# Two-layer decoder, state-space stage: side work of ScalarE and VectorE placed by half units

## The reference, cut to what matters

```python
for i in range(nl):                                  # 4
    h = _rms(x, norm_w[i])
    xz = jnp.einsum('bld,ed->ble', h, W_in[i])
    xi, z = jnp.split(xz, 2, axis=-1)
    xp = jnp.pad(xi, ((0, 0), (dc - 1, 0), (0, 0)))
    xc = conv_b[i] + sum((xp[:, k:k + L, :] * conv_w[i][:, k] for k in range(dc)))
    xc = _silu(xc)
    dbc = jnp.einsum('bld,ed->ble', xc, W_x[i])
    delta, Bm, Cm = jnp.split(dbc, [rk, rk + n], axis=-1)
    delta = jax.nn.softplus(jnp.einsum('blr,dr->bld', delta, W_dt[i]) + b_dt[i])
    A = -jnp.exp(A_log[i])
    deltaA = jnp.exp(delta[..., None] * A)
    BX = (delta * xc)[..., None] * Bm[:, :, None, :]
    _, hs = jax.lax.associative_scan(combine, (deltaA, BX), axis=1)
    y = jnp.einsum('bldn,bln->bld', hs, Cm) + D[i] * xc
    out = jnp.einsum('bld,ed->ble', y * _silu(z), W_out[i])
    x = x + out
```

## Time and profile before

| what | value |
|---|---|
| median of 3 runs | 1283.86 us (1282.17 to 1284.41) |
| the profiled execution, its own time | 1286.74 us |
| span of its profile | 1285.0 us |
| busy share of the span: PE, DVE, ACT, POOL | 88%, 82%, 64%, 60% |
| mean granted TensorE clock | 0.949 of full speed |

### The profile page before, as it was taken

The page is one execution under the profiler, slowest core; times in us unless marked ns, Lnnn a source line. Parts: engine busy times, 40 slices in busy tenths (PEclk is TensorE's granted clock), DMA queues, the critical chain, the costliest instruction groups (busy, mean ns, idle before and its releaser), DMA issues.

```text
span 1285.0 us, 17476 instructions
## 1 busy us (share of the span) xinstructions
PE 1128.5 (88%) x5960; PEld 660.0 (51%) x5960; DVE 1050.3 (82%) x1642; ACT 825.1 (64%) x1816; POOL 775.4 (60%) x641
## 2 busy tenths in 40 slices
PE   7798888879759998998998999989989689999974
PEld 3455555544325454554554545545545346666643
DVE  4577777675689999999999999999999985676657
ACT  1455555655466786777767767877776436788763
POOL 6001111100389898998998999989989952554202
PEclk9899999998979999999998999989999899999878
DMA  7000002000510600502404107014042003100000
GB/s 211 13 13 13 13 13 73 2 1 3 201 44 0 217 34 2 205 17 88 162 1 181 42 1 251 1 54 168 1 150 88 1 11 90 34 18 18 2 1 26
DMA packets 22141, 79.13 MB, mean 62 GB/s; under 512 B 4935, under 2 KB 8847, under 8 KB 21138
## 3 DMA queue, kind: packets, MB, share of 16 engines
q1 hardware_dynamic: 22054, 78.02, 17.7%
HBM read 76.77 MB, written 1.24 MB: 61 GB/s over the span
## 4 chain that ended last, share of the span: by engine, by line
PE 42%; DVE 33%; ACT 10%; POOL 8%; issue 7%; DMA 0%; DVEq 0%; SPq 0%; POOLq 0%; ACTq 0%
PE ps L675 38%; DVE ps L2089 10%; DVE arena L2094 6%; DVE arena L2092 5%; POOL arena L2003 4%; PE ps L744 4%; ACT ps L1886 2%; DVE hstat L1213 2%; POOL arena L2015 2%; DVE arena L2052 2%; ACT L670 1%; DVE arena L1189 1%; ACT arena L936 1%; DVE arena L1179 1%; ACT arena L1776 1%
## 5 line engine op out<-in xcount | busy, mean ns | idle before, releaser
L675 PE MATMUL ps<-arena 128*32 128x100 f32 (+10 forms) x3330 | 517.4, 380 | 67.3 <-ACT arena L936 14.6
L2003 POOL TENSOR_TENSOR arena<-arena 128x1600 f32<-128x1600 f32 x128 | 456.6, 3582 | 34.0 <-DVE ps L2089 25.8
L675 PE MATMUL ps<-arena,ident 128*128 128x400 f32 x1024 | 386.5, 528 | 29.4 <-POOL arena L2015 19.9
L675 PEld LDWEIGHTS ps<-arena 128*32 128x32 f32 (+7 forms) x3330 | 259.4, 144 | 294.3 <-issue 115.9
L1886 ACT ACTIVATE ps<-arena 128x400 f32<-128x400 f32 x512 | 282.9, 589 | 184.5 <-DVE arena L2092 151.3
L2089 DVE TENSOR_TENSOR_SCAN ps<-ps,arena 128x800 f32<-128x800 f32 x176 | 320.6, 1822 | 22.8 <-ACT ps L1886 17.1
L675 PEld LDWEIGHTS ps<-arena,ident 128*128 128x128 f32 x1024 | 201.5, 200 | 196.4 <-issue 28.3
L642 POOL TENSOR_SCALAR stat<-stat 100x1 f32<-100x1 f32 (+1 forms) x44 | 8.5, 193 | 419.9 <-DVE stat L623 419.0
L2092 DVE TENSOR_TENSOR arena<-ps,arena 128x800 f32<-128x800 f32 x176 | 174.5, 991 | 6.0
L2015 POOL TENSOR_TENSOR arena<-arena 128x1600 f32<-128x1600 f32 x40 | 143.1, 3579 | 16.8 <-DVE arena L2094 16.7
L2094 DVE TENSOR_TENSOR_SCAN arena<-ps,arena 128x800 f32<-128x800 f32 x80 | 140.3, 1803 | 0.9 <-ACT ps L1886 0.7
(11 more groups left out here) (199 smaller groups left out, 1025.7 us busy)
## 6 DMA issues: line engine op xcount, KB each, us to landing
arena<-bc_scratch SPq DMA_DIRECT2D x64, 800.0 KB, 6.4
arena<-in_ctxT SPq DMA_DIRECT2D x16, 361.0 KB, 4.0
arena<-in_w_in SPq DMA_DIRECT2D x4, 1024.0 KB, 5.0
arena<-in_expT SPq DMA_DIRECT2D x1, 2048.0 KB, 12.9
arena<-in_w_out SPq DMA_DIRECT2D x4, 512.0 KB, 3.2
arena<-in_mask SPq DMA_DIRECT2D x8, 141.0 KB
arena<-in_xT SPq DMA_DIRECT2D x2, 400.0 KB, 4.1
x_tok<-in_x_tok SPq DMA_DIRECT2D x1, 800.0 KB
```

The lines of the kernel that those rows point to most:

```text
L675: return nc.tensor.matmul(outp, lhsT, rhs, start=first, stop=last)
L2003: nc.gpsimd.tensor_tensor(bx[:, unit % BX].rearrange("p (j t) -> p j t", j=SEGMENT), bbc[:, nq].rearrange("p (j t) -> p j t", j=SEGMENT), ...
```

## The change

The table's entries are now places between halves: n.0 is after the first half of unit n, n.5 after its second, so an old n is a new n.5. ScalarE's and VectorE's loops run over 32 halves. The copy of O0, O1 (`am_keep`) gets an entry of its own. TensorE's and GpSimd's places (`p...`, `g...`) stay.

| step | before (as a place) | after |
|---|---|---|
| squares `aQ` | 4.5 | 3.0 |
| scaling `aH` | 5.5 | 5.0 |
| keep `aHk` | 5.5 | 6.0 |
| skip diagonal `aK` | 2.5 | 4.5 |
| taps `aG` | 5.5, 6.5 | 4.5, 5.5 |
| rates `aA` (exp of A_log) | 10.5 | 9.0 |
| convolution on VectorE `vC` | 10.5 | 10.0 |
| silu `aS` | 11.5 | 11.0 |
| copy of DB `aB` | 12.5 | 12.0 |
| softplus `aD` | 13.5, 14.5 | 13.0, 14.5 |
| y(3) on VectorE | 16.5 | 16.0 |
| `aV`, `aT`, `aX`, `aY`, `aC`, `aZ`, y(0) to y(2) | n.5 | the same |

```diff
-    "aK": 2,
-    "aQ": 4,
+    "aQ": 3.0,
+    "aV": 3.5,
     "gN": 4,
-    "aH": 5,
+    "aK": 4.5,
+    "aG": {2: 4.5, 3: 5.5},
+    "aH": 5.0,
+    "aHk": 6.0,
     "pT": 7,
-    "aT": 6,
+    "aT": 6.5,
     "pX": (9, 9, 8, 8, 15, 15, 16, 16),
-    "aG": (5, 6),
-    "aX": 7,
-    "aY": 8,
-    "aC": 9,
-    "vC": 10,
-    "aZ": (15, 15, 16, 16),
-    "aV": 3,
-    "aS": 11,
+    "aX": 7.5,
+    "aY": 8.5,
+    "aC": 9.5,
+    "vC": 10.0,
+    "aS": 11.0,
     "pB": 11,
-    "aB": 12,
+    "aB": 12.0,
     "pD": (12, 12, 14, 14),
-    "aD": (13, 14),
-    "aA": 10,
+    "aD": (13.0, 14.5),
+    "aZ": (15.5, 15.5, 16.5, 16.5),
+    "aA": 9.0,
     "gA": 15,
     "gD": (14, 15, 16, 17),
-    "vY": (5, 10, 13, 16),
+    "vY": (5.5, 10.5, 13.5, 16.0),
...
+                for k in range(2 * UNITS):
+                    if m or k >= 2:
+                        am_half(act, 2 * UNITS * m + k)
+                    am_between(act, m, k / 2)
+                    if m + 1 == ROUNDS and k % 2:
+                        guest_act(act, k // 2)
...
-                        vm_unit(dve, UNITS * m + u)
...
+                for k in range(2 * UNITS):
+                    unit, h = UNITS * m + k // 2, k % 2
+                    if m or k >= 2:
+                        if h == 0:
+                            wait(dve, m_red, unit - HS + 1)
+                            dve.wait_ge(m_bx, unit + 1)
+                        vm_half(dve, unit, h)
...
                     for c in range(CD):
-                        if u == AT["vY"][c]:
+                        if k / 2 == AT["vY"][c]:
                             vm_y(dve, m, c)
-                        if m and u == AT["vY"][c] - UNITS:
+                        if m and k / 2 == AT["vY"][c] - UNITS:
                             vm_y(dve, m - 1, c)
```

More of the change, by code:

```diff
@@ L1022, in act_attn @@
                     if g == AHEAD["aU"]:
-                        am_unit(act, 0)
+                        am_half(act, 0)
+                        am_half(act, 1)
                     for b in fin(g, AT["MT"]):
@@ L1777, in am_scale @@
             last.then_inc(m_h, 1)
-            if m >= 2:
-                am_keep(act, m - 2, g, 0)
-                am_keep(act, m - 2, g, 1)
         def am_turned(act, m):
@@ L1866, in am_skip, with am_half @@
             last.then_inc(m_skip, 1)
-        def am_unit(act, unit):
+        def am_half(act, k):
+            unit, h = divmod(k, 2)
             m, u = divmod(unit, UNITS)
@@ L1872, in am_unit @@
             l, g = divmod(m, G)
-            if nq == 0:
+            if nq == 0 and h == 0:
                 act.wait_ge(m_first, CD * m + c + 1)
@@ L1876, in am_unit @@
                     act.wait_ge(m_aneg, l + 1)
[L1877 to L1888, removed]
+            if k >= 2:
+                before, bh = divmod(k - 2, 2)
+                if on_dve(before):
+                    act.wait_ge(m_cmd, dve_halves(before, bh))
+                else:
+                    act.wait_ge(m_scan, k - 1)
+            for j in range(2):
+                n = c * NS + nq * SEGMENT + 2 * h + j
+                last = nc.scalar.activation(psf[:, half_at(k) + j * GT:half_at(k) + (j + 1) * GT],
+                                            delta[g][:, c], ACT.Exp, scale=aneg[:, l % 2, n:n + 1])
+            last.then_inc(m_exp, 1)
         def mam_act(act):
@@ L1892, in mam_act @@
             for m in range(ROUNDS):
[L1893 to L1946, removed]
@@ new lines, in mam_act, with am_between @@
+                for k in range(2 * UNITS):
[4 more added lines that the diff above has]
+                        guest_act(act, k // 2)
+        def am_between(act, m, at):
+            l, g = divmod(m, G)
+            ng = 1 - g
+            for c in range(CD):
+                if m and at == AT["aZ"][c] - UNITS:
+                    am_z(act, m, g, c)
+            if at == AT["aV"]:
+                table(act, SET_SILU)
+                am_silu_z(act, m, g)
+                table(act, SET_EXP_LN)
+            if at == AT["aK"] and g == 0:
+                am_skip(act, m, l)
+            if m + 1 == ROUNDS:
+                if at == AT["aHk"]:
+                    am_keep(act, m - 1, ng, 0)
+                    am_keep(act, m - 1, ng, 1)
+                return
+            if at == AT["aQ"]:
+                am_square(act, m + 1, ng)
+            if at == AT["aH"]:
+                am_scale(act, m + 1, ng)
+            if at == AT["aHk"] and m + 1 >= 2:
+                am_keep(act, m - 1, ng, 0)
+                am_keep(act, m - 1, ng, 1)
+            if at == AT["aT"]:
+                am_turned(act, m + 1)
+            for c in (2, 3):
+                if at == AT["aG"][c] and (m == 0 or g == 1):
+                    am_taps(act, m, l + g, c)
+            for c in (2, 3):
+                if at == AT["aX"]:
+                    am_raw_x(act, m + 1, ng, c)
+            for c in (2, 3):
+                if at == AT["aY"]:
+                    am_conv_out(act, m + 1, ng, c)
+            for c in range(2):
+                if at == AT["aC"]:
+                    am_conv(act, m + 1, ng, c)
+            for c in range(CD):
+                if at == AT["aZ"][c]:
+                    am_z(act, m + 1, ng, c)
+            if at == AT["aS"]:
+                table(act, SET_SILU)
+                am_silu(act, m + 1, ng)
+                table(act, SET_EXP_LN)
+            if at == AT["aB"]:
+                am_dbc(act, m + 1)
+            for k in range(2):
+                if at == AT["aD"][k]:
+                    table(act, SET_SOFTPLUS)
+                    for c in (2 * k, 2 * k + 1):
+                        am_soft(act, m + 1, ng, c)
+                    table(act, SET_EXP_LN)
+            if at == AT["aA"] and g == 1:
+                am_rates(act, l + 1)
@@ L2094, in vm_half @@
                 nc.vector.tensor_tensor_scan(y, a, bx[:, unit % BX, w], 0.0, ALU.mult, ALU.add).then_inc(m_scan, 1)
[L2096 to L2100, removed]
         def vm_y(dve, m, c):
@@ L2114, in mam_dve @@
             for m in range(ROUNDS):
[L2115 to L2118, removed]
-                        vm_unit(dve, UNITS * m + u)
-                    if m + 1 == ROUNDS:
-                        guest_dve(dve, u)
+                for k in range(2 * UNITS):
[5 more added lines that the diff above has]
+                        vm_half(dve, unit, h)
+                    if m + 1 == ROUNDS and h == 1:
+                        guest_dve(dve, k // 2)
                     for c in range(CD):
-                        if u == AT["vY"][c]:
+                        if k / 2 == AT["vY"][c]:
                             vm_y(dve, m, c)
-                        if m and u == AT["vY"][c] - UNITS:
+                        if m and k / 2 == AT["vY"][c] - UNITS:
                             vm_y(dve, m - 1, c)
-                    if m + 1 < ROUNDS:
-                        if u == AT["vC"]:
-                            vm_conv(dve, m + 1, ng, 0)
+                    if m + 1 < ROUNDS and k / 2 == AT["vC"]:
+                        vm_conv(dve, m + 1, 1 - m % G, 0)
             vm_y(dve, ROUNDS - 1, CD - 1)
```

## The result

| | before | after |
|---|---|---|
| median | 1283.57 us (4 runs, 1282.17 to 1284.41) | 1327.99 us (4 runs, 1323.79 to 1336.23) |
| ratio | | 1.0355, 95% interval 1.0304 to 1.0406 |
| profiled execution, its own time and span | 1286.74, 1285.0 us | 1323.79, 1322.1 us |
| TensorE's mean granted clock | 0.949 | 0.933 |

The change costs 44 us. The forecast was slower, 1316 us within 1297 to 1334: sign and range hold, the size was 12 us short. In the changed kernel the lines have moved: scans are L2097 and L2102 (were L2089, L2094), products L2100, y L2112 (L2110), exponentials L1885 (L1886), table loads L671, matmuls L676, GpSimd's products L2011 and L2023.

The account below looks back on a forecast made before the run. VectorE's queue was taken as the scan stage's clock, a round being 83.1 us plus waits; terms summed to +32.9, giving 1319.6 from 1286.74 or 1316.8 from the median, stated as 1316, range 1297 to 1334.

Parts of the forecast that it names:

- squares to 3.0: ScalarE's squares after unit 3's first half lengthen the wait before unit 4 by 1.44 in rounds 1 to 6: +8.6 us.
- softplus D0, D1 to 13.0: Two table loads and two activations delay VectorE's second half of unit 13 by 1.71 in rounds 0 to 6: +12.0 us.
- y(3) to 16.0: VectorE reaches y(3) before TensorE's sums are done and waits 2.9, of which 0.1 is old; seven times 2.8: +19.6 us.
- rest before unit 15: Unit 15 still waits some 0.2 for its exponential in each of seven rounds: +1.4 us.
- clock, put before unit 15: TensorE at half speed around unit 12's sum makes it and D2 late; 0.5 a round taken between 0 and 1.0: +3.5 us.
- waits before y(2), unit 7, unit 15 gone: Old VectorE waits that disappear: -3.6 before y(2), -1.95 before unit 7 in odd rounds, -6.7 before unit 15.
- the gate of two halves: PSUM has two halves for exponentials, so the exponential of half k starts only when half k-2 is done.
- the second rival: A half-clock dip of 6.8 us falls into TensorE's chain before y(3): +21 us more, 1337 us; chance 0.11.
- a dip half in the chain: Case within the forecast: the half-clock stretch lies partly in TensorE's chain before y(3), giving 1330 us.
- The faster rival: ScalarE leads by more than two halves, steps at 3.0 and 13.0 hide, only the removed 12.3 us count: about 1272; chance 0.04.
- the merging of waits: Waits at 13.5 and 16.0 give the others the time they lacked, gain and loss balance: 1284 us; chance 0.03.
- a cover of 0.8 us: TensorE's output matmuls after y(3) end 9.5 us after y starts; the squares' third read comes at about 10.3.

Follow-up runs that it names:

- Without the four moves: Changed kernel with y(3) back at 16.5, first softplus pair at 13.5, squares at 4.5, copy of O0, O1 at 5.5: 1277.95 us, ratio 0.996.

## Why the prediction was right, and where it was short

| step of the prediction | forecast | measured in the trace |
|---|---|---|
| squares to 3.0 | +8.6 | 2.38 for 1.04 and 0.88: +8.5 |
| round 0 | 0 | 91.7 for 90.9 us, which is its softplus wait less its old wait before unit 15, both in other rows: 0 |
| softplus D0, D1 to 13.0 | +12.0 | 7 x 1.53 = +10.7 |
| y(3) to 16.0 | +19.6 | 35.1 less 0.6: +34.5 |
| rest before unit 15 | +1.4 | 0 |
| clock, put before unit 15 | +3.5 | none there; 14.9 of the row of y(3) |
| waits before y(2), unit 7, unit 15 gone | -12.3 | all gone: -12.3 |
| round 7, copy of O0, O1 | 0 | +2.75 |
| unit 10 of round 5 (half clock) | 0 | +1.5 |

The measured column adds up to 45.7, against 44.7 for the stage; where the 1.0 is saved is not shown.

**Squares and softplus** were sized by the gate of two halves, and the runs that move each alone or back confirm the places and the sizes. The softplus step was 0.18 too dear (1.53 a round for 1.71).

**y(3)**: the step was "TensorE running 42 matmul records without a break" against VectorE half a unit earlier. At full clock it is exact: 2.85 to 3.04 with y(3) alone and with the softplus back. The term that was mis-sized is the clock. The forecast took 0.5 a round, "the distance between 1.27 and 0.73", and placed it at unit 12, before the softplus. The runs showed it inside the chain, at X4 and X5, at 1.6 us a round and 3.2 in two: the second rival's mechanism, at 14.9 us where 21 was given there (its 3 us a round assumed the long stretch each time). That is 14.9 us where the sum had 3.5, nearly all of the 12 us that the forecast was short. The idle time was also elsewhere than forecast: unit 11's sum itself ran at half clock (5.60 us) and filled the gap before unit 12, and the 2.00 us before X4 preceded the second low stretch. The argument against that rival, that the chain ran at full clock before, did not carry: the early softplus changes what TensorE does ahead of it (2.00 us idle before X4 with it, 0.71 without), and with the softplus back the chain is at full clock in all seven rounds. Why a stretch falls to half clock in one place and not in another is not shown; the 3.15 us of the run with the softplus back did not bring it.

The range held because it was drawn wide enough for a part of rival 2: "a dip half in the chain gives 1330" is what came. The forecast of 1316 itself had the dip at the wrong place.

**The copy to 6.0** was costed at nothing on ScalarE's queue. What failed is that it was not asked who waits for it: in round 7 GpSimd does, with b times x behind it, and VectorE behind that. In the kernel before, VectorE sat idle 0.16 us at that place.

**The faster rival and the merging of waits** fall: beyond what the sum already had, waits did not replace each other within a round, with the one exception of y(3) and the squares, which share O1. That link was in the prediction as a cover of 0.8 us, and the run with y(3) back used it up.

**What gained** was costed rightly in the changed kernel: all 12.3 us of old waits are gone. But a part of that came from the costly moves: of the 6.7 before unit 15, 4.0 come back with the softplus at 13.5. Without the four moves the gain is 6.6 us.

## What to carry to other kernels

Price a step not by its length but by the gate on either side of it: with two buffers, a step of length s behind item k fits if two items' work of the consumer covers two productions and s. Here the softplus step at 13.0 had 1.76 + 2.76 us of VectorE's work against 2 x 1.11 + 3.69: short by 1.39 without the small gaps, 1.53 measured. Before short items a step fits less well. Where a product waits for the end of a long unbroken chain, its place is set by where that chain starts, and moving the consumer ahead alone only makes a wait; look for who reads what the consumer makes as well, since the loss can move there. A new wait ahead of TensorE's work can cost twice, once as the wait and once as half clock in a chain that others wait for; here it did, and only a run with that one step back showed it.

## What was not expected of the hardware

The step that made VectorE wait 1.53 us a round cost 3.0 (21 us in seven rounds): with it, TensorE's clock was 0.50 for 3.3 us in the chain of 14.4 us, and without it 1.00 throughout. Between rounds of one execution it was the length of the half-clock stretch in the chain that differed (3.4 or 6.8 us). The four runs of the changed kernel spread over 12 us and the first four of the kernel before over 2, but 19 later ones of the kernel before went from 1275.35 to 1291.51, so a wider spread is not shown. In one of the fourteen profiles the granted clock stood at 0.95 between the low stretches from the start of the execution to its end, where all others had 1.00; its cause is open.
